# A graph network on one core: the edge step with its feature products as one group, and a last stage with rings of six pairs

## The reference

```python
edge_index = jnp.stack([src, dst])            # row = src, col = dst
# layer 0: mean over neighbours, two products, a gate by node
h_mean = (x + mean_neighbor) * 0.5 @ W_mean + b_mean
h_concat = concat([x @ W_ego + b_ego, mean_neighbor @ W_nb + b_nb])
x = _layernorm(x + (1 - gate) * h_mean + gate * h_concat)
# layer 1, for each of 4 heads:
feats = jnp.maximum(x @ w1 + bb1, 0.0) @ w2 + bb2          # 256 -> 256 -> 64
x_cat = concat([feats[row], feats[col], elem[:, None]])     # 129
e1 = leaky_relu(jnp.maximum(x_cat @ a1 + aab1, 0.0) @ a2 + aab2)
w = jnp.exp(e1 - jnp.max(e1))
pooled = segment_sum(w[:, None] * feats[col], row)
head = pooled / (segment_sum(w, row) + 1e-10)[:, None]
x = _layernorm(x + concat(heads))
```

## Time and profile before

| what | value |
|---|---|
| median of three runs | 3639.89 us |
| profiled run | 3619.23 us |
| its span, first to last instruction | 3617.5 us |
| PE busy, of the span | 3155.7 us (87%) |
| DVE busy | 2649.3 us (73%) |
| ACT busy | 1849.6 us (51%) |
| POOL busy | 1772.2 us (49%) |
| edge step, first turn to last turn (L1417) | 1449.7 to 3219.2 us |
| first to last put (L1562) | 3300.2 to 3606.9 us |

### The profile page before, as it was taken

The page is one execution under the profiler, slowest core; times in us unless marked ns, Lnnn a source line. Parts: engine busy times, 40 slices in busy tenths (PEclk is TensorE's granted clock), DMA queues, the critical chain, the costliest instruction groups (busy, mean ns, idle before and its releaser), DMA issues. The chain is left out here.

```text
span 3617.5 us, 57511 instructions
## 1 busy us (share of the span) xinstructions
PE 3155.7 (87%) x15761; PEld 2191.4 (61%) x15761; DVE 2649.3 (73%) x8931; ACT 1849.6 (51%) x4206; POOL 1772.2 (49%) x1691
## 2 busy tenths in 40 slices
PE   6777878878889896799999999999999999995765
PEld 3444555545555554577777777777777777772333
DVE  7776766664444445588888888888888888877876
ACT  3454655555555555344444444444444444434765
POOL 2555465646666662544444444444444444403665
PEclk9998989999999998899999999999999999997898
DMA  5777887665556555433333333333333333315775
GB/s 156 256 243 263 300 273 263 208 207 194 200 189 205 198 202 192 125 117 116 115 116 116 116 116 117 114 117 114 115 116 116 116 115 117 116 42 173 229 228 170
DMA packets 289095, 597.09 MB, mean 165 GB/s; under 512 B 41326, under 2 KB 198810, under 8 KB 288950
## 3 DMA queue, kind: packets, MB, share of 16 engines
q1 hardware_dynamic: 206662, 360.13, 29.8%
q0 software_dynamic: 75744, 232.45, 20.2%
q10 hardware_dynamic: 6544, 2.89, 0.3%
HBM read 287.39 MB, written 322.05 MB: 168 GB/s over the span
## 5 line engine op out<-in xcount | busy, mean ns | idle before, releaser
L1207 POOL TENSOR_TENSOR u_hc<-u_hc 128x1536 f32<-128x1536 f32 x98 | 270.4, 2759 | 768.6 <-DVE u_h L1317 749.2
L1027 PE MATMUL bank<-w_node,xT 128*128 128x384 f32 x1564 | 600.8, 514 | 14.5 <-ACT bank L627 14.0
L1429 PE MATMUL bank<-xh,w1h 128*128 128x512 f32 x1568 | 538.0, 424 | 19.3 <-DVE xl L1346 14.5
L1259 ACT ACTIVATE hidT<-bank,b1c 128x512 f32<-128x512 f32 x392 | 268.5, 685 | 516.6 <-PE bank L1429 508.0
L1429 PE MATMUL bank<-xh,w1l 128*128 128x512 f32 x1568 | 493.9, 396 | 0.0
L1429 PE MATMUL bank<-xl,w1h 128*128 128x512 f32 x1568 | 493.4, 396 | 0.0
L1340 DVE TENSOR_SCALAR hidT<-bank,b1c 128x512 f32<-128x512 f32 x392 | 293.7, 749 | 216.0 <-PE bank L1429 211.7
L732 DVE SCALAR_TENSOR_TENSOR H<-bank,gates,X 128x256 f32<-128x256 f32 x391 | 187.3, 479 | 316.5 <-remote 164.6
L1027 PEld LDWEIGHTS bank<-w_node,xT 128*128 128x128 f32 x1564 | 295.0, 202 | 179.1 <-issue 23.1
L1443 PE MATMUL bank<-hidT,w2f 128*64 128x256 f32 x3136 | 381.7, 385 | 10.1 <-issue 10.1
L1355 DVE STREAM_TRANSPOSE feat<-catT 32x256 f32<-32x256 f32 x784 | 342.6, 437 | 17.1 <-ACT catT L1268 3.0
(11 more groups left out here) (278 smaller groups left out, 6254.8 us busy)
## 6 DMA issues: line engine op xcount, KB each, us to landing
hc_tab<-H SPq DMA_DIRECT2D x78, 960.0 KB
er<-edge_tab SPq DMA_DIRECT2D x98, 512.0 KB
X<-in_x SPq DMA_DIRECT2D x78, 640.0 KB
out_x<-O SPq DMA_DIRECT2D x78, 640.0 KB
hc_tab<-zero_row SPq DMA_DIRECT2D x10, 4032.0 KB
hc_tab<-zero_row SPq DMA_DIRECT2D x9, 3840.0 KB
edge_tab<-u_x SPq DMA_DIRECT2D x98, 256.0 KB, 2.2
edge_tab<-feat SPq DMA_DIRECT2D x98, 256.0 KB, 2.2
```

The source lines that it names most:

```text
L1027: ins = t_.matmul(p[:, 0:384], xT[t // 2 % XR][:, t % 2, c * P:(c + 1) * P], w_node[:, c, :], start=False, stop=c == 1, skip_group_check=True)
L1207: g.tensor_tensor(c, c, u_hc[s][:, :, MULT:MULT + 3].unsqueeze(3).to_broadcast([P, 4, 3, P]), ALU.mult).then_inc(u_scaled, 1)
L1259: a.activation(hidT[m][:, :], bank[2 + m % 2][:, :], ACT.Relu, bias=b1c[:, m:m + 1])\
L1429: ins = t_.matmul(bank[2 + m % 2][:, :], w[:, c, m * P:(m + 1) * P], xx[s][:, c, :], start=n == 0, stop=n == 5)
```

## The change

In the edge step:
- TensorE's features(0) and features(1) of a pair stand together, behind hidden_0 of the next pair. The group waits once, for all eight relus and for ScalarE's reads of both banks. As hidT[0] is then read later, ScalarE's relu(0) waits until both are done.
- ScalarE's order begins with seed_0 and features_0 (now lag 3), then relu_0, features_1.
- VectorE's feat_1 moves from the end of its step to behind stat one step later (lag 4), and feat_0 behind scale.
- SP issues keep_f (now lag 4) ahead of keep_x.

In the last stage:
- the rings of er, val, agg, zo, their semaphores and the banks go from four pairs to six (banks 2 to 7); the mending's results share bank 1.
- lags: VectorE stat, aggr, variance 2 to 3, scale and shift 3 to 4; ScalarE root 2 to 3, norm 3 to 5. norm waits once a pair instead of twice. GpSimd's put goes from lag 2 to 0, with nothing else in its stream.
- tail is made in `finish`, inside VectorE's last full step, behind add.

```diff
-                skewed(sp, US, 2, [(keep_x, 0), (keep_f, 1)])
+                skewed(sp, US, 2, [(keep_f, 4), (keep_x, 0)])
...
                 def relu(u, m):
                     act.wait_ge(w1_ready, u * 8 + (m + 1))
+                    if m == 0 and after(u, 1):
+                        act.wait_ge(w2_ready, u * 2)
...
-                skewed(act, US, 2, [(relu_0, 2), (features_1, 3), (seed_0, 3), (root, 0), (relu_2, 2), (norm, 0),
-                                    (relu_4, 2), (seed_1, 3), (high, 1), (relu_6, 2), (features_0, 2)])
+                skewed(act, US, 2, [(seed_0, 3), (features_0, 3), (relu_0, 2), (features_1, 3), (root, 0), (relu_2, 2),
+                                    (norm, 0), (relu_4, 2), (seed_1, 3), (high, 1), (relu_6, 2)])
...
-                skewed(dve, US, 2, [(stat, 0), (relu_1, 2), (feat_0, 3), (scale, 0), (relu_3, 2), (dots_0, 3),
-                                    (relu_5, 2), (low, 1), (dots_1, 3), (feat_1, 3), (relu_7, 2)])
+                skewed(dve, US, 2, [(stat, 0), (feat_1, 4), (relu_1, 2), (scale, 0), (feat_0, 3), (relu_3, 2),
+                                    (dots_0, 3), (relu_5, 2), (low, 1), (dots_1, 3), (relu_7, 2)])
...
                 def features(u, k):
-                    pe.wait_ge(act_hid, u * 4 + 2 * k + 2)
-                    pe.wait_ge(dve_hid, u * 4 + 2 * k + 2)
-                    if after(u, 1):
-                        pe.wait_ge(cat_ready, u * 4 + 2 * k - 2)
+                    if k == 0:
+                        pe.wait_ge(act_hid, u * 4 + 4)
+                        pe.wait_ge(dve_hid, u * 4 + 4)
+                        if after(u, 1):
+                            pe.wait_ge(cat_ready, u * 4)
...
-                def features_1(u, s):
+                def features_0_1(u, s):
+                    features(u, 0)
                     features(u, 1)
...
-                skewed(pe, US, 2, [(hidden_0, 1), (features_1, 2), (hidden_1, 1), (hidden_2, 1), (scores_0, 2),
+                skewed(pe, US, 2, [(hidden_0, 1), (features_0_1, 2), (hidden_1, 1), (hidden_2, 1), (scores_0, 2),
                                    (hidden_3_4, 1), (turn, 0), (hidden_5, 1), (scores_1, 2), (hidden_6, 1),
-                                   (features_0, 1), (hidden_7, 1)])
+                                   (hidden_7, 1)])
...
-        SL = 8
-        SLOTS = [len(range(q, ET, SL)) for q in range(SL)]
-        SP2 = SL // 2
-        LASTQ = (ET - 1) % SL
-        Z0 = 3
+        RING = 6
+        SLOTS = [len(range(s, ET // 2, RING)) for s in range(RING)]
+        LASTS = (ET // 2 - 1) % RING
+        Z0 = 2
...
-                    if after(u, SP2):
-                        sp.wait_ge(z_seeded, u - (SP2 - 1))
-                        sp.wait_ge(val_ready, u - (SP2 - 1))
+                    if u >= RING:
+                        sp.wait_ge(z_seeded, u - (RING - 1))
+                        sp.wait_ge(val_ready, u - (RING - 1))
...
-                straight(ET, SL, [(put, 2)])
+                straight(ET, 2, [(put, 0)])
...
                 def norm(u, s):
                     act.wait_ge(znb, u + 1)
+                    if u >= RING:
+                        act.wait_ge(zo_out[s], u // RING * 32 + IN0[s])
                     for k in range(2):
                         q = 2 * s + k
-                        if after(u, SP2):
-                            act.wait_ge(zo_out[q], (u - s) * 4 + IN0[q])
...
-                straight(ET // 2, SP2, [(root, 2), (seed, 0), (choose, 0), (norm, 3)])
+                straight(ET // 2, RING, [(root, 3), (seed, 0), (choose, 0), (norm, 5)])
...
-                straight(ET // 2, SP2, [(stat, 2), (weigh, 0), (aggr, 2), (scale, 3), (add, 0), (variance, 2),
-                                           (shift, 3)])
-
-                dve.wait_ge(agg_ready, ET)
-                v.tensor_tensor(tail[:, :].rearrange("p (h f) -> p h f", h=HEADS),
-                                agg[LASTQ // 2][:, LASTQ % 2, :].rearrange("p (h f) -> p h f", h=HEADS),
-                                fix_w[:, 1, :].unsqueeze(2).to_broadcast([P, HEADS, FEAT]), ALU.mult)\
-                    .then_inc(tail_ready, 1)
+                def finish(u, s):
+                    if u == ET // 2 - 1:
+                        dve.wait_ge(agg_ready, ET)
+                        v.tensor_tensor(tail[:, :].rearrange("p (h f) -> p h f", h=HEADS),
+                                        agg[LASTS][:, 1, :].rearrange("p (h f) -> p h f", h=HEADS),
+                                        fix_w[:, 1, :].unsqueeze(2).to_broadcast([P, HEADS, FEAT]), ALU.mult)\
+                            .then_inc(tail_ready, 1)
+
+                straight(ET // 2, RING, [(stat, 3), (weigh, 0), (aggr, 3), (scale, 4), (add, 0), (finish, 0), (variance, 3),
+                                         (shift, 4)])
```

More of the change, by code:

```diff
@@ L1513, in build @@
         mxa = tmp("mxa", [P, HEADS])
[L1514 to L1517, removed]
+        er = [tmp(f"er{s}", [P, 2, 2 * D]) for s in range(RING)]
+        val = [tmp(f"val{s}", [P, 2, D]) for s in range(RING)]
+        agg = [tmp(f"agg{s}", [P, 2, D]) for s in range(RING)]
+        zo = [tmp(f"zo{s}", [P, 2, D]) for s in range(RING)]
         pick = [tmp(f"pick{b}", [P, P]) for b in range(4)]
-        z_st, z_mv = tmp("z_st", [P, SL, 6]), tmp("z_mv", [P, SL, 2])
-        z_v, z_d, z_r, z_b = (tmp(n, [P, SL]) for n in ("z_v", "z_d", "z_r", "z_b"))
+        z_st, z_mv = tmp("z_st", [P, 2 * RING, 6]), tmp("z_mv", [P, 2 * RING, 2])
+        z_v, z_d, z_r, z_b = (tmp(n, [P, 2 * RING]) for n in ("z_v", "z_d", "z_r", "z_b"))
         fix_e, fix_z, fix_o = tmp("fix_e", [P, 2 * D]), tmp("fix_z", [P, D]), tmp("fix_o", [P, D])
@@ L1531, in build @@
              "fix_var fix_sd fix_nb fix_o_ready fix_o_out").split())
-        er_in = [sem(f"er_in{s}") for s in range(SP2)]
+        er_in = [sem(f"er_in{s}") for s in range(RING)]
         z_opened, z_seeded = sem("z_opened"), sem("z_seeded")
-        zo_out = cn_out[0:SL]
-        IN0 = [(len(range(2 * q, ET, RS)) + len(range(2 * q + 1, ET, RS))) * 16 for q in range(SL)]
+        zo_out = cn_out[0:RING]
+        IN0 = [(len(range(2 * q, ET, RS)) + len(range(2 * q + 1, ET, RS))) * 16 for q in range(RING)]
         pair_rows = edge_tab.rearrange("b p d -> (b p) d")
@@ L1559, in put @@
                 def put(t, q):
+                    s = t // 2 % RING
                     pool.wait_ge(zo_ready, t + 1)
@@ L1570, in _ @@
                     .then_inc(fo_out, 16)
-                for q in range(SL):
-                    pool.wait_ge(zo_out[q], SLOTS[q] * 16 + IN0[q])
+                for s in range(RING):
+                    pool.wait_ge(zo_out[s], SLOTS[s] * 32 + IN0[s])
                 pool.wait_ge(fo_out, 16)
@@ L1655, in _ @@
                 st.done(v.tensor_reduce(fix_w[:, 0, :], w_end[:, :, :], AX.X, ALU.add))
-                st.done(v.memset(agg[SP2 - 1][:, 1, :], 0.0))
+                st.done(v.memset(agg[RING - 1][:, 1, :], 0.0))
                 st.wait()
@@ L1668, in weigh @@
                 def weigh(u, s):
-                    dve.wait_ge(er_in[s], (u - s) * 4 + 16)
-                    if after(u, SP2):
-                        dve.wait_ge(agg_ready, u * 2 - 6)
+                    dve.wait_ge(er_in[s], u // RING * 16 + 16)
+                    if u >= RING:
+                        dve.wait_ge(agg_ready, 2 * (u - RING) + 2)
                     dve.sem_inc(dve_hop, 1)
@@ L1707, in scale @@
                     dve.wait_ge(zsd, u + 1)
-                    if after(u, SP2):
-                        dve.wait_ge(zo_ready, u * 2 - 6)
+                    if u >= RING:
+                        dve.wait_ge(zo_ready, 2 * (u - RING) + 2)
                     v.reciprocal(z_r[:, 2 * s:2 * s + 2], z_d[:, 2 * s:2 * s + 2]).then_inc(zr, 1)
@@ L1732, in _ @@
                 st.wait()
-                st.done(v.tensor_tensor(fix_z[:, :], bank[2][:, 0:D], fix_z[:, :], ALU.add))
+                st.done(v.tensor_tensor(fix_z[:, :], bank[1][:, 0:D], fix_z[:, :], ALU.add))
                 st.done(v.reciprocal(fix_w[:, 1, :], fix_w[:, 0, :]))
@@ L1755, in _ @@
                 t_ = nc.tensor
-                for s in range(SP2):
+                for s in range(RING):
                     ins = t_.matmul(bank[Z0 + s][:, :], ident[:, :], bias_all[:, :], start=True, stop=True)
@@ L1773, in heads @@
                                   skip_group_check=True).then_inc(head_used, 1)
-                straight(ET // 2, SP2, [(join, 0), (heads, 0)])
+                straight(ET // 2, RING, [(join, 0), (heads, 0)])
                 pe.wait_ge(tail_ready, 1)
-                t_.matmul(bank[2][:, 0:D], earlier_same[:, :], tail[:, :], start=True, stop=True)
-                t_.matmul(bank[1][:, 0:HEADS], earlier_same[:, :], w_sum[:, ET - 1, :], start=True, stop=True)\
-                    .then_inc(sums_ready, 1)
+                t_.matmul(bank[1][:, 0:D], earlier_same[:, :], tail[:, :], start=True, stop=True,
```

(3 more changed lines are left out.)

28 lines of the change are left out of this document (13 added, 15 removed).

## The result

In the comparison on record the changed kernel takes 3584.83 us (median of four runs, 3578.09 to 3594.45), the kernel before 3639.73 (four runs, 3622.53 to 3644.17): a ratio of 0.9847, interval 0.981 to 0.9884. The profiled executions lie closer, 3594.45 against 3619.23: the one after is the longest of its four, and the one before, which is not among the four, is shorter than all of them.

| stretch, us | before | after | forecast |
|---|---|---|---|
| start to first turn (not changed) | 1449.7 | 1468.3 | 0 |
| first turn to last turn, 97 steps | 1769.5 | 1725.6 | -42 |
| one round, median | 17.98 | 17.63 | 17.63 |
| last turn to first add | 69.1 | 66.9 | -0.3 |
| first add to first put | 11.9 | 14.3 | +2 |

What follows compares the result with a forecast made beforehand. TensorE was taken to bound the edge step, VectorE's stops to hold the last stage, where no engine is full. 3619.23 - 34.3 - 8 - 0.3 + 3.5 = 3580.1, plus 20.7 gives 3601 us; own range 3590 to 3612, outer 3582 to 3622.

Steps and rivals of the forecast that it cites:

- The bound of the edge step, TensorE: Edge step: TensorE, busy 1472.37 of 1481.00 us, binds; time spared there comes off until VectorE's chain binds.
- One group, 34.3 us: Edge step, TensorE: joining two feature groups saves an entry, an exit and a ramp, 0.35 us a round over 98 rounds.
- ramp inside the group: TensorE's feature group: 0.16 us beyond its matmul rhythm (1.88 - 8 x 0.215), saved once a round by joining.
- relu_7 within 0.1 us of the features: Edge step: VectorE's relu_7 just makes TensorE's features, under 0.1 us to spare; rival of missing it, 3665 us, chance 0.08.
- relu_0, scores_0, the seeds: Edge step: the reordering's new waits for ScalarE's relu_0, features_1 and score-bank seeds stay hidden behind TensorE's other work.
- Stores, 0: Edge step, SP: two stores a round change places, each landing in about 2 us, no engine waiting; 0, bounds -1 and +2.
- Late starts, -8: Edge step: relu_5's late starts on VectorE, tied to GpSimd's fetches, go, -8 us; rival that they stay, chance 0.13.
- Drain, -0.3: End of the edge step: the seed no longer stands behind the last feature copy, gaining 0.3 us.
- Rings of six, 0: Last stage: deeper rings gain 0, since VectorE's stops hold the chain; bounds 0 and -49 us.
- Longer lags, +3.5: Last stage: +5.1 us in the drain, -2.4 in front, +0.8 for the tail product; sum +3.5, bounds -2 and +8.
- The offset of 20.7: Whole run: the median shown, 3639.89 us, lies 20.7 above the profiled run; added to the forecast sum.
- rings that pay: Rival, last stage: VectorE's stops are passed on less and GpSimd's 49 us of waits vanish, 3552 us; chance 0.07.

Runs made afterwards that it cites:

- rings_only: Edge step of the kernel before with the changed last stage (rings of six, longer lags, early tail); 3334.02 us, ratio 1.0 to the kernel before.
- group_only: Changed TensorE and ScalarE orders, but VectorE's and SyncE's orders and the last stage of the kernel before; 3472.8 us against 3335.14 before.
- turn_by_scores: Changed kernel with TensorE's two transposes (turn) moved directly behind the first score transposes; 3330.78 us, ratio 0.9989 to the kernel before.
- edge_only_2: Repeat in the third comparison: changed edge step with the last stage of the kernel before; 3300.64 us, ratio 0.9897 to the kernel before.
- short_lags_2: Repeat in the third comparison: changed kernel with rings of six but the last-stage lags of before; 3297.76 us, ratio 0.9891 to the kernel before.
- after_again: The whole change repeated unaltered in the first comparison of the experiments; 3300.39 us, ratio 0.9896 to the kernel before.
- edge_only: Changed edge step with the last stage of the kernel before, first comparison of the experiments; 3299.63 us, ratio 0.9897 to the kernel before.
- after_third: The whole change repeated unaltered in the third comparison of the experiments; 3301.71 us, ratio 0.9904 to the kernel before.

## Why the prediction was right, point by point

- **The bound of the edge step, TensorE.** Right: busy 1480.92 of 1481 us, and every saved piece came off the round.
- **One group, 34.3 us.** Right, and shown free of other terms by the pair rings_only and whole change: 34.0. The pieces add up rightly to 0.35, but the 0.16 read as a ramp inside the group is 0.05 at its start and 0.11 more of the exit. Their cause is the 64-column form: padded to 128 columns, the group has none of the three.
- **relu_7 within 0.1 us of the features.** The mechanism held, the size was off: relu_7 ends 0.27 us ahead of the features where the prediction had 0.18, 0.11 of it for the semaphore in either case, since the stretch from relu_5 took 4.71 and not 4.80. group_only shows the price of missing it, 1.67 us of waiting a round.
- **relu_0, scores_0, the seeds.** Hidden, as costed: TensorE has 0.1 us without work in 1481. turn_by_scores shows how near: its seeds come 0.2 us late.
- **Stores, 0.** Right in the sum, with one size wrong. SyncE's store of a pair's rows is issued at 2523.18, 0.17 us behind the end of norm (ScalarE, 2520.94 + 2.07). It takes 5.4 us to land in place of the 2.2 before and the 2 of the prediction, and no engine waits for it; the page's row:

```profile
edge_tab<-u_x SPq DMA_DIRECT2D x98, 256.0 KB, 5.4
```

- **Late starts, -8.** The one step whose reason failed in part. In the profiles of record the rounds' excess over their median, from the third round on, fell from 11.5 to 1.5 us, so the term came out at -10, beyond its bound of -9, which was read from a window of 82 rounds. That the fetches move away from relu_5 is so: they end 1.6 to 1.7 us ahead of it after the change. The one late round behind the start has a fetch that was itself held up and ended next to relu_5 (GpSimd's and VectorE's timeline, after):

```profile
2419.68 0.94 POOL L1197 DMA_INDIRECT u_hc<-hc_tab,u_idx  x1 [0.30 <-issue]
```
```profile
2420.68 0.75 DVE L1342 TENSOR_SCALAR hidT<-bank,b1c 128x512 f32<-128x512 f32 x1 [1.47 <-PE bank L1431]
```

  But the end of a fetch alone delays nothing: rings_only has it at the same place and no late start, so there was nothing to remove, and the edge step gains 34.0 us and no more. Whether VectorE's order removed the late starts in the comparison on record was not tried by itself, and what delays relu_5 there stays open.
- **Drain, -0.3.** 2.2 between the two profiles of record, 0.2 between rings_only and the whole change (68.2 and 68.0).
- **Rings of six, 0.** Right: 54.4 us of waits in place of 49.1 there, and 1.0 (0.9991 to 1.0009) for rings and longer lags together in rings_only. With the lags left short the rings are worth 3 us at most (edge_only_2 and short_lags_2).
- **Longer lags, +3.5.** Right in kind; first put 2.4 us later, +0.6 from the last turn to the end there, +1.5 and +1.2 against the last stage of before in the later comparisons (after_again and edge_only, after_third and edge_only_2). The drain was mis-sized as a term of its own: the last pair's add to the last put went from 13.7 to 22.2 us, 8.5 more where 5.9 were forecast (5.1 and 0.8), and the stretch before it was 5.9 shorter, since VectorE only runs further ahead of the puts.
- **The offset of 20.7.** It was added to go from the profiled execution to the median. The median after came 9.6 us under its profiled one instead, and the stage that nothing changed differed by 18.6 between the two executions. 3601 was 16 us over 3584.83: without the offset the sum of 3580.1 lies 4.7 from it, by chance of the same noise. So 3584.83 lies below 3590 to 3612, the forecast's own range, and inside the outer one, 3582 to 3622, whose lower end was left for rings that pay. They did not; that the time fell inside is luck, while the terms of the stages are right as said above.

## What to carry to other kernels

On an engine that is busy without a gap, look at the distances between starts at each place where the shape of its work changes: two groups of 64-column matmuls cost 0.35 us more than one, and no idle time or busy share shows that. Before joining groups, follow the last input of the joint group on the other engines: here a 1.8 us piece of VectorE's had to move first, or the gain of 34 us would have been a loss of over 130. Where the last engine of a chain is the bound, make it start early: deeper rings with longer lags only let the others run further ahead.

## What the hardware showed that I had not expected

Two 64-column matmuls run side by side at 0.216 us each; padded to 128 columns the group's 16 steps of 0.216 us became 32, and the kernel went from 0.9896 to 1.0807 of the time before.

The kernel before took 305 us more in the comparison on record than in the comparisons of the experiments (3639.73 and 3333 to 3335), and not evenly: the stage ahead of the edge step takes 1468.3 us in the first profile after and 1220.7 in after_again, the last stage 398.8 and 354.2, the edge step 1725.6 and 1724.6. Windows of that first stage, after and after_again:

```profile
0.00:1450.00 1450.00, 1163.95 (x4969) 733.38 (x4969) 865.82 (x3297) 765.78 (x1751) 776.61 (x808) 0.93 0.65 220
```
```profile
0.00:1200.00 1200.00, 1081.13 (x4965) 702.79 (x4965) 863.88 (x3297) 773.20 (x1751) 776.11 (x806) 0.97 0.79 266
```

VectorE, ScalarE and GpSimd do the same work in the same busy time; the same traffic moves at 220 GB/s in the one and 266 in the other, and the edge step, at 119 GB/s, does not differ. That points at the way to memory, by the chip or by what ran beside it; no run here tells which. A gain of 54.9 us in one comparison was 33.9 and 31.4 in two others.
